# Decoder layer on one core: x2 of batches 4 and 5 turned by VectorE in 32x32 blocks, queues reordered

## The reference

```python
x = _layernorm(x + _L0_attn_ref(x, Wq, Wk, Wv, Wo))       # 16 heads of 64, rotary, causal
x = _layernorm(x + _L0_xattn_ref(x, ctx_4096))            # softmax(x ctx^T) ctx, one head of 1024
x = _layernorm(x + _L0_ffn_ref(x, weight, bias, A, B, starts))   # x W^T + bias + a LoRA by batch
```

## Time and profile before

| what | value |
| --- | --- |
| median of 3 runs | 523.33 us |
| profiled execution, its time | 522.58 us |
| its span, first to last instruction | 520.60 us |
| granted TensorE clock, mean | 0.996 |
| TensorE busy | 513.0 us (99%) |
| VectorE busy | 319.8 us (61%) |
| ScalarE busy | 262.6 us (50%) |
| GpSimd busy | 152.1 us (29%) |
| chain that ended last | TensorE 98%, DMA 1% |
| TensorE's waits | 1.6 us in all |
| share of the chain in turn_row (L726) | 1.2%, eight turns |

### The profile page before, as it was taken

One profiled execution on the slowest core, in us unless ns is written; L12 is line 12 of the kernel. 1 busy time (PEld: TensorE's weight loads), 2 busy tenths in 40 slices (PEclk: granted clock), 3 DMA queues, 4 the chain that ended last, 5 costly groups with the idle time before them and its releaser, 6 DMA issues.

```text
span 520.6 us, 7823 instructions
## 1 busy us (share of the span) xinstructions
PE 513.0 (99%) x2864; PEld 438.4 (84%) x2864; DVE 319.8 (61%) x693; ACT 262.6 (50%) x664; POOL 152.1 (29%) x139
## 2 busy tenths in 40 slices
PE   8999999999999999999999999999999999999995
PEld 5888888888989888888978888888887888988884
DVE  5822000187776868677674797769887776845432
ACT  5713210183856648384565356357868464525231
POOL 0003500536353554742006150113937000110010
PEclk9999999999999999999999999999999999999998
DMA  8907612331021111100095677579987477333011
GB/s 284 320 16 180 184 40 82 126 118 51 32 69 55 42 40 43 42 2 0 1 280 162 146 205 210 148 200 262 263 247 212 133 207 214 104 91 110 1 75 47
DMA packets 37958, 65.60 MB, mean 126 GB/s; under 512 B 4872, under 2 KB 20616, under 8 KB 37920
## 3 DMA queue, kind: packets, MB, share of 16 engines
q1 hardware_dynamic: 37248, 64.58, 43.1%
q10 hardware_dynamic: 672, 0.52, 0.3%
HBM read 54.08 MB, written 3.67 MB: 111 GB/s over the span
## 4 chain that ended last, share of the span: by engine, by line
PE 98%; DMA 1%; ACT 0%; DVE 0%; SPq 0%; issue 0%; ACTq 0%
PE bank L539 30%; PE bank L656 30%; PE bank L550 15%; PE bank L742 6%; PE bank L566 3%; PE bank L581 3%; PE bank L773 2%; PE bank L775 2%; PE bank L778 2%; PE bank L726 1%; PE bank L715 1%; DMA x_raw<-x_feat 1%; PE bank L687 1%; PE bank L793 1%; PE bank L689 1%; PE bank L796 1%
## 5 line engine op out<-in xcount | busy, mean ns | idle before, releaser
L539 PE MATMUL bank<-x_hi,w_hi 128*128 128x512 f32 (+1 forms) x256 | 93.7, 366 | 0.0
L539 PE MATMUL bank<-x_hi,w_lo 128*128 128x512 f32 (+1 forms) x256 | 93.2, 364 | 0.0
L539 PE MATMUL bank<-x_lo,w_hi 128*128 128x512 f32 (+1 forms) x256 | 93.1, 364 | 0.0
L1386 DVE STREAM_TRANSPOSE prob_t<-prob 32x256 f32<-32x256 f32 x160 | 69.7, 436 | 12.1 <-ACT prob L947 9.4
L656 PE MATMUL bank<-wo,act_hi 128*128 128x512 f32 x224 | 70.2, 395 | 0.0
L656 PE MATMUL bank<-ffn,act_hi 128*128 128x512 f32 x224 | 70.0, 394 | 0.0
L1755 POOL TENSOR_TENSOR w_lo<-w_mix,w_hi 128x1024 fp32r<-128x1024 f32 x16 | 38.3, 2396 | 104.6 <-ACT w_hi L922 104.6
L937 ACT ACTIVATE prob<-prob,shift 112x112 f32<-112x112 f32 x128 | 47.8, 378 | 40.8 <-DVE shift L1369 40.8
L1768 POOL TENSOR_TENSOR norm<-norm,minus_half 128x1 f32<-128x1 f32 (+1 forms) x22 | 16.8, 765 | 156.5 <-DVE norm L1459 156.5
L539 PEld LDWEIGHTS bank<-x_hi,w_hi 128*128 128x128 f32 x256 | 48.1, 188 | 6.0
L539 PEld LDWEIGHTS bank<-x_lo,w_hi 128*128 128x128 f32 x256 | 48.1, 188 | 5.1
(11 more groups left out here) (119 smaller groups left out, 960.6 us busy)
## 6 DMA issues: line engine op xcount, KB each, us to landing
cf_raw<-ctx_feat SPq DMA_DIRECT2D x32, 376.0 KB, 4.1
ct_raw<-ctx_tok SPq DMA_DIRECT2D x24, 448.0 KB
w_raw<-qkv_w SPq DMA_DIRECT2D x16, 512.0 KB, 3.4
half_raw<-wo_w SPq DMA_DIRECT2D x16, 256.0 KB, 5.8
half_raw<-ffn_w SPq DMA_DIRECT2D x16, 256.0 KB, 7.0
wv_raw<-qkv_w SPq DMA_DIRECT2D x15, 256.0 KB, 7.2
x_raw<-x_feat SPq DMA_DIRECT2D x7, 448.0 KB, 8.1
out<-y_t SPq DMA_DIRECT2D x6, 512.0 KB, 3.9
```

Of the source, the lines that this page charges most:

```text
L539: last = pe.matmul(to[:, 0:cols.stop - cols.start], a[:, k, :], b[:, k, cols], start=(k == 0 and b is x_hi and a is w_hi[w]), stop=(k == K ...
L1386: return dve.transpose(quads(prob_t_wide[r], key, query), quads(prob_wide[r], query, key))
```

## The change

The turns b4 and b5 leave TensorE. In their place VectorE turns the rows of x2 of these two batches itself, by 16 transposes of 32 rows x 256 elements a batch (4 row quadrants x 4 feature quadrants, each instruction taking eight 32x32 blocks), written to SBUF where the features belong, into act_raw, which lies where act_lo lies. round_blocks (ScalarE) makes act_hi out of it and rest_blocks (VectorE) act_lo in place.

A batch has 112 rows, and four quadrants are 128: the last 16 columns that are written belong to the next batch, whose x1 is no longer needed, and are zeros, since GpSimd clears rows 96 to 127 of the three row buffers once, after the heads. copy_row waits for that.

```diff
-TURNS = ["a0", "a1", "a2", "b0", "a3", "b1", "a4", "b2", "a5", "b3", "a6", "b4", "b5", "b6", "b7"]
+TURNS = ["a0", "a1", "a2", "b0", "a3", "b1", "a4", "b2", "a5", "b3", "a6", "b6", "b7"]
+BLOCKS = range(4, 6)
...
+            def turn_blocks(b):
+                dve.wait_ge(x2_ready, b + 1)
+                for q in range(QUADS):
+                    t = b * S + QUAD * q
+                    for d in range(QUADS):
+                        last = dve.transpose(act_raw[QUAD * d:QUAD * d + QUAD, :, t:t + QUAD],
+                                             row_all[b % ROWS][QUAD * q:QUAD * q + QUAD, :].rearrange(
+                                                 "p (k d i) -> p k d i", k=KT, d=QUADS)[:, :, d, :])
+                last.then_inc(swapped, 1)
+
+            def rest_blocks(b):
+                for c in range(2):
+                    ks = slice(4 * c, 4 * c + 4)
+                    dve.wait_ge(block_rounded, 2 * blocks_before(b) + c + 1)
+                    dve.tensor_tensor(act_lo[:, ks, tokens_of(b)], act_raw[:, ks, tokens_of(b)],
+                                      act_hi[:, ks, tokens_of(b)].bitcast(F32),
+                                      ALU.subtract).then_inc(block_rest, 1)
...
+            def round_blocks(b):
+                act.wait_ge(swapped, blocks_before(b) + 1)
+                for c in range(2):
+                    ks = slice(4 * c, 4 * c + 4)
+                    act.activation(act_hi[:, ks, tokens_of(b)], act_raw[:, ks, tokens_of(b)],
+                                   ACT.Copy).then_inc(block_rounded, 1)
...
@@ TensorE @@
-                pe.wait_ge(turn_rest, 2 * AT_TURN[f"b{i + 1}"] + 2)
+                if i + 1 in BLOCKS:
+                    pe.wait_ge(block_rest, 2 * blocks_before(i + 1) + 2)
+                else:
+                    pe.wait_ge(turn_rest, 2 * AT_TURN[f"b{i + 1}"] + 2)
...
-            turn_row(4)
...
-            turn_row(5)
...
@@ GpSimd @@
+            pool.wait_ge(heads_done, 2 * PAIRS)
+            pool.wait_ge(wo_rest, 2 * NB)
+            for i in range(ROWS):
+                pool.memset(row_all[i][P - QUAD:P, :], 0.0).then_inc(rows_set, 1)
+                pool.wait_ge(rows_set, i + 1)
...
@@ ScalarE: the second half of V's weights is waited for four loads at a time @@
-                act.wait_ge(wv_in[c][k], 16)
+                if c == 0:
+                    act.wait_ge(wv_in[0][k], 16)
+                else:
+                    act.wait_ge(wv_in[1][k // 4], 64)
```

More of the change, by code:

```diff
@@ L186, in build @@
                                            + [cf_at[3] + 2048 * i for i in range(3)])]
-        row = [at(f"row{i}", [S, D], (Q0 + 24576, S0 + 12288, S0 + 16384)[i]) for i in range(ROWS)]
+        row_all = [at(f"row{i}", [P, D], (Q0 + 24576, S0 + 12288, S0 + 16384)[i]) for i in range(ROWS)]
+        row = [r[0:S, :] for r in row_all]
         a_both = at("a_both", [P, KT, SECOND + RA], S0 + 20480, F32R)
@@ L243, in build @@
         x_rounded, x_rest = sem("x_rounded"), sem("x_rest")
-        wv_in = [[sem(f"wv_in{c}_{k}") for k in range(KT)] for c in range(2)]
+        wv_in = [[sem(f"wv_in0_{k}") for k in range(KT)], [sem(f"wv_in1_{h}") for h in range(2)]]
         wv_rounded, wv_rest = sem("wv_rounded"), sem("wv_rest")
@@ L1142, in _ @@
             round_ct(7)
+            round_ct(8)
             keep_cprob_t(1)
-            round_ct(8)
             round_ct(9)
@@ L1158, in _ @@
             round_ct(13)
+            round_ct(14)
             keep_cprob_t(2)
-            round_ct(14)
             round_ct(15)
@@ L1165, in _ @@
             round_turned("b1")
+            round_ff(2)
+            norm_x1(4)
             round_cf(15)
-            norm_x1(4)
-            round_ff(2)
+            round_cf(16)
             round_ff(3)
-            round_cf(16)
             round_ff(4)
@@ L1173, in _ @@
             round_ct(17)
+            cross_exp(3)
             round_ff(5)
-            cross_exp(3)
             round_ff(6)
             round_ff(7)
+            round_cf(18)
+            round_turned("a4")
             norm_x1(5)
-            round_turned("a4")
-            round_cf(18)
             round_ct(18)
@@ L1205, in _ @@
             round_ct(24)
+            round_ct(25)
             keep_t_part(0)
             norm_x2(3)
-            round_ct(25)
             round_ct(26)
@@ L1212, in _ @@
             round_ct(28)
+            keep_y(1, 0)
             keep_cprob_t(4)
-            keep_y(1, 0)
             round_turned("b3")
@@ L1232, in _ @@
             keep_y(1, 1)
-            round_turned("b4")
             round_cf(27)
-            norm_y(1)
             round_cf(28)
+            round_blocks(4)
             round_cf(29)
             round_ct(35)
+            round_cf(30)
             cross_exp(6)
-            round_cf(30)
             round_ct(36)
+            round_ct(37)
             keep_t_part(1)
-            norm_x2(5)
-            round_ct(37)
             round_ct(38)
-            keep_y(2, 0)
             round_ct(39)
             round_ct(40)
+            norm_x2(5)
+            keep_y(2, 0)
+            keep_y(3, 0)
             keep_cprob_t(6)
-            keep_y(3, 0)
-            round_turned("b5")
             round_cf(31)
             keep_y(2, 1)
+            round_blocks(5)
             round_ct(41)
             cross_exp(7)
-            norm_y(2)
+            norm_y(1)
             round_ct(42)
+            round_ct(43)
             norm_x2(6)
-            round_ct(43)
+            round_ct(44)
             keep_cprob_t(7)
-            round_ct(44)
             round_ct(45)
@@ L1266, in _ @@
             round_ct(47)
+            norm_y(2)
             norm_y(3)
@@ L1591, in _ @@
             add_wo(6)
+            cross_top(0)
             rest_turned("a1")
-            cross_top(0)
+            rest_cf(4)
             rest_ct(0)
-            rest_cf(4)
             rest_ct(1)
+            rest_cf(5)
             rest_ct(2)
-            rest_cf(5)
             rest_cf(6)
@@ L1631, in _ @@
             rest_ct(13)
+            rest_cprob_t(2)
             add_wo(11)
-            rest_cprob_t(2)
             rest_ct(14)
@@ L1636, in _ @@
             rest_ct(16)
+            rest_turned("b1")
             rest_cf(15)
-            rest_turned("b1")
+            rest_cf(16)
+            cross_top(3)
             add_wo(12)
-            cross_top(3)
             rest_ct(17)
-            rest_cf(16)
             rest_cf(17)
@@ L1656, in _ @@
             rest_cf(20)
-            rest_cf(21)
             cross_top(4)
             rest_ct(23)
+            rest_cf(21)
             add_row(3)
@@ L1670, in _ @@
             measure_y(0, 0)
+            rest_turned("b3")
             measure_y(1, 0)
-            rest_turned("b3")
             rest_cf(23)
@@ L1681, in _ @@
             rest_cf(26)
+            turn_blocks(4)
+            rest_cf(27)
             rest_ct(30)
@@ L1687, in _ @@
             rest_ct(34)
-            measure_y(1, 1)
-            rest_turned("b4")
-            rest_cf(27)
+            rest_ct(35)
+            rest_blocks(4)
+            cross_top(6)
             rest_cf(28)
             rest_cf(29)
-            cross_top(6)
-            rest_ct(35)
+            rest_cf(30)
             add_row(5)
-            rest_cf(30)
             mask_t(1)
@@ L1700, in _ @@
             rest_ct(38)
+            rest_cprob_t(6)
+            turn_blocks(5)
+            rest_cf(31)
             rest_ct(39)
-            rest_cprob_t(6)
             rest_ct(40)
-            measure_y(2, 0)
-            measure_y(3, 0)
-            rest_turned("b5")
-            rest_cf(31)
-            measure_y(2, 1)
             cross_top(7)
+            rest_blocks(5)
             rest_ct(41)
+            measure_y(1, 1)
             add_row(6)
             rest_ct(42)
+            measure_y(2, 0)
             rest_ct(43)
+            measure_y(3, 0)
+            rest_ct(44)
             rest_cprob_t(7)
-            rest_ct(44)
             rest_ct(45)
             rest_ct(46)
+            measure_y(2, 1)
             measure_y(3, 1)
```

81 lines of the change are left out of this document (46 added, 35 removed).

## The result

The changed kernel took 525.81 us (median of 7 runs, 524.98 to 527.26), the kernel before, on the same chip, 523.15 (522.48 to 524.16): a ratio of 1.0055, 95% interval 1.0039 to 1.0071. It is slower by 2.7 us, where 0.9 was forecast, and its median lies 0.1 above the range.

The account below looks back on a forecast made before the run. TensorE, busy 513.0 of 520.6 us, was taken to bound the kernel. -1.54 + 1.2 + 1.25 = +0.9 on the profiled 522.58 gave 523.5; the median 0.75 above it, 524.2, range 522.1 to 525.7.

Parts of the forecast that it names:

- What goes, 1.54 us: On TensorE, turn_row(4) and turn_row(5), 0.77 us of the chain each, come off the end: -1.54 us.
- The transposes, 7.2 us a batch: On VectorE, 16 transposes of 32x256 a batch, a step of 0.452 us: 7.2 us, bounds 5.1 to 7.3.
- Batch 4 free: Batch 4's transposes on VectorE delay no matmul; the blocks reach ffn(3,0) with 0.5 us to spare.
- First new wait, tile 2: mask_t(1) ahead of add_low(2,0): t_part behind ct 37's load makes TensorE wait 0.6 to 1.2 us, 1.2 taken.
- the second half of that step's argument: At tile 2, even with ct 37's load landed, VectorE starts mask_t(1) late behind add_row(5): 0.7 us late.
- Second new wait, cf 31: rest_cf(31), behind batch 5's transposes on VectorE, ahead of cross_score(7, last): load 1.3 us after its old time, 1.25 in the sum.
- Elsewhere, -0.5 to +1.4, taken as 0: Other moved operations, among them cf 15, t_part(0) behind ct 25 and ct 23: together -0.5 to +1.4 us, 0 taken.
- a landing near 399.9: ct 25's load, ahead of keep_t_part(0) on ScalarE, lands then: up to 0.9 us more, or 0.3 less.
- The memsets and V's weights: Three GpSimd memsets, 7.2 us at most in a 10.38 gap, cost nothing; V's weights wait by fours, ScalarE idling afterwards.
- Rival 2: Landing order decides three times: cf 15 +0.65, ct 25 +0.85, giving 525.7; chance 0.40 with the forecast's side above 524.38.
- the signs announced: TensorE waits for t_both near 446 (0.6 to 1.2 us) and cf_lo near 458 (1 or more), both behind VectorE.

Follow-up runs that it names:

- experiment 5: Changed kernel with the early order of before, a new late order, and batch 5's transposes in two halves behind rest_cf(31): 527.53 us, ratio 1.0077.
- experiment 13: 9 with measure_y(2,1) and measure_y(3,1) moved behind rest_ct(47) on VectorE: 521.22 us, ratio 0.9972 against the kernel before.
- experiment 11: Kernel before with one line moved, mask_t(0) ahead of rest_cf(22) on VectorE, no blocks: 522.44 us, ratio 0.9991.
- experiment 10: Only batch 4 by blocks, in the order of experiment 5, batch 5 turned by TensorE, mask_t(0) ahead of rest_cf(22): 522.02 us, ratio 0.9982.
- experiment 4: Changed kernel with keep_t_part(1) ahead of round_ct(37) on ScalarE and turn_blocks(5) behind rest_ct(40) on VectorE: 528.65 us, ratio 1.011.
- Experiment 3: Changed kernel's order on every queue without its blocks, x2 of batches 4 and 5 turned by TensorE again: 526.48 us, ratio 1.0062.
- experiment 2: Changed kernel with everything up to x2 of batch 3 in the order of the kernel before, on all four engines: 524.36 us, ratio 1.0026.
- experiment 8: Kernel before with only the semaphores of V's weights, the three memsets and copy_row(0,0) behind them: 523.06 us, ratio 0.9998.
- 9: experiment 5 with round_blocks(5) ahead of round_ct(42) and (43) on ScalarE, and mask_t(0) ahead of rest_cf(22) on VectorE: 523.63 us, ratio 1.0013.

## Why the prediction was wrong, step by step

**What goes, 1.54 us: right in the trace.** ffn(3,0) came 0.87 nearer to its old time with nothing but turn_row(4) taken out in between, and experiment 5 stood 1.3 us ahead of the kernel before until 457.26. By the medians, experiment 13 is 1.2 under experiment 11 for both turns, and experiment 10 0.4 for one.

**The transposes, 7.2 us a batch: right** (7.18 us for sixteen, 435 ns the median). The Trainium skill (VectorE: DVE Perf Modes, The three transpose paths) gives 311 ns a 128x128 in bf16. The sixteen turn eight such blocks, so in fp32 two of them make one: 0.90 us, and the trace goes on disagreeing. The prediction's 1.8 us for a 128x128 is twice too long; its sum used the 7.2 us a batch and was not touched.

**Batch 4 free: right.** No wait at cf 27 or ffn(3,0); the second rest of the blocks ended at 442.30, 0.56 ahead of the load at 442.86, where 0.5 was forecast.

**First new wait, tile 2: right in place and cause, too small in size: 1.6, where 0.6 to 1.2 was given and 1.2 taken.** t_part was copied at 449.18, behind ct 37, which had waited for its load, and by VectorE's own queue (add_row(5) ends at 448.8) it could have been masked 0.8 earlier; experiment 4 left 0.69, as the second half of that step's argument said (0.7).

**Second new wait, cf 31: right in place and cause, 0.85 against 1.25.** TensorE's step from one matmul to the next was 1.02 there instead of 0.23, and the start of the next was 0.06 longer. It came later than forecast, because all before it did, and so did the loads that TensorE releases. Experiment 3 shows that it is the transposes' own, experiment 13 that it is only their place's. That the two waits together came to 2.45, as forecast, is luck: one was 0.4 more and the other 0.4 less.

**Elsewhere, -0.5 to +1.4, taken as 0: this step failed.** By the trace these places cost 3.4 us: cf 15 0.63, cf 19 0.69 and tile 0 2.06. By the medians it is about 1.45 (experiment 2) of the 1.8 us by which the forecast was short of the measured difference; the late part, 1.5 by the medians where 0.9 was forecast, covers the rest. Four mistakes made it so. First, t_part(0) behind ct 25 was given a lateness of 0.9 at most by a landing near 399.9; in the changed kernel's trace the load landed in time for 402.56:

```profile
402.56 0.63 ACT L1058 ACTIVATE ct_hi<-ct_raw 125x512 fp32r<-125x512 f32 x1 [1.24 <-DMA ct_raw<-ctx_tok]
403.21 0.38 ACT L1123 ACTIVATE t_part<-bank 48x256 f32<-48x256 f32 x1
```

That load is issued only when TensorE has used the buffer, from 394.76 instead of 393.38, as TensorE was 1.5 us late by then. Second, no row has a landing near 399.9: the earlier trace rows say only that ct 25 was there when ScalarE came to it at 401.08, and one trace is one sample. The same swap at ct 37 had been costed with care. Third, VectorE's subtractions were costed at 0.93 wherever they stood. With the ffn subtractions moved, cf 21's met GpSimd's in all five traces with the early order of the change (2.02 to 2.04 us), and cf 22's in the four where it stands ahead of the mask (1.83 to 1.97). In the early order of before cf 22's took 0.93 to 0.95 in four traces of six, 1.99 and 3.20 in the others. The changed kernel (cf 21, cf 22):

```profile
393.70 2.04 DVE L1583 TENSOR_TENSOR cf_lo<-cf_raw,cf_hi 128x752 fp32r<-128x752 f32 x1
...
400.15 1.97 DVE L1583 TENSOR_TENSOR cf_lo<-cf_raw,cf_hi 128x752 fp32r<-128x752 f32 x1
```

Fourth, cf 19 has no term in the sum at all. Its load stood behind four of ffn there, issued at 381.57, and took 5.7 us; before, it was issued at 380.47 and landed after 3.6. From the chain that led to the wait:

```profile
381.57 5.72 DMA cf_raw<-ctx_feat
387.32 0.84 ACT cf_hi L1046
388.19 1.53 DVE cf_lo L1583
```

Of the three early places only cf 15 stayed inside its bounds, 0.63 of 0 to 0.65, rounded at 366.50 behind norm_x1(4) as the prediction feared. Of the five traces with this early order all have a wait for cf 15 (0.2 to 0.8) and two one for cf 19 (0.5 and 0.7); the ten with the early order of before, or all but a line of it, have neither.

**The memsets and V's weights cost nothing: right** (experiment 8; 2.97 us of memsets, done at 293.6).

**The rivals.** Rival 2, the landing order deciding three times, named cf 15 and tile 0 and came to 525.7, 0.1 from what was measured. Its places are right, its number in part luck: it gave tile 0 0.85 where the trace has 2.06, and left out cf 19. It had been given less than the forecast, on the ground that the ffn loads move into half-empty time; but cf 19's load, behind them, took 2.1 us longer, and for tile 0 ScalarE's queue, TensorE's release of the load and GpSimd decided. Of the signs announced, the places and the causes were there, the sizes not quite: TensorE stood still for 1.3 us for t_both, at 451 (0.6 to 1.2 near 446), and for 0.6 for cf 31, at 463 (1 or more near 458). None of the signs looked at the places ahead of 429.

**What stays open.** The trace's early waits make 3.4 us and the medians 1.45. Executions of one kernel differ by 1.4 us and more, and there is one trace of each kernel, so how often each wait occurs in it is not known. Nor was it separated whether cf 15 and cf 19 cost something by themselves when tile 0 doesn't wait, nor what the late order of experiments 10 and 13 is worth without blocks.

## What to carry to other kernels

Where one engine is busy 98% of the span, moving work off it pays one for one, but only if no urgent operation of the taker's queue ends up behind the new work: take the list of what the busy engine waits for, and put the new work behind the last urgent item, in pieces if need be. In experiments 4, 9 and 13 two lines of order moved the time by 2.8, 3.9 and 2.4 us, each more than the 1.54 that the change could win; part of the first two is the clock, which fell in experiments 4 and 5. Cost each swap that puts a wait for a load ahead of a small urgent copy at the load's landing in a bad execution, not at the one in the trace.
